# One fused image-and-text transformer block on one core: the opening's transfers and first products, a bank in the expert loop, and the last tile's way to the result

## The reference

```
h = concat(class_token, patches @ W.T + b) + pos_embed      # 16 x 197 x 192
h = concat(h, txt)                                         # 16 x 325 x 192
q, k, v = split(layernorm(h) @ W_qkv + b_qkv)
h = h + ((q @ k.T) / sqrt(192) * decay_mask) @ v
y = layernorm(h)                                           # 5200 rows
sig = sigmoid(y @ Wg.T)                                    # 128 experts
top 6 of sig + e_bias per row; weights sig / sum * 2.5
expert e takes at most its first 192 rows:
  routed += w * ((silu(y @ gate_e) * (y @ up_e)) @ down_e) # inner width 464
shared = (silu(y @ Wsg) * (y @ Wsu)) @ Wsd                 # inner width 928
result = h + routed + shared
```

## Time and profile before

| | us |
|---|---|
| median of 3 runs | 711.11 |
| the profiled execution's own time | 710.25 |
| its span, first to last instruction | 708.6 |
| TensorE busy in the span | 675.0 (95%) |
| VectorE (DVE) busy | 471.5 (67%) |
| ScalarE (ACT) busy | 331.9 (47%) |
| GpSimd (POOL) busy | 210.5 (30%) |
| mean granted TensorE clock | 0.988 |

### The profile page before, as it was taken

The page is one execution under the profiler, slowest core; times in us unless marked ns, Lnnn a source line. Parts: engine busy times, 40 slices in busy tenths (PEclk is TensorE's granted clock), DMA queues, the critical chain, the costliest instruction groups (busy, mean ns, idle before and its releaser), DMA issues.

```text
span 708.6 us, 16559 instructions
## 1 busy us (share of the span) xinstructions
PE 675.0 (95%) x4587; PEld 630.5 (89%) x4588; DVE 471.5 (67%) x1486; ACT 331.9 (47%) x803; POOL 210.5 (30%) x312
## 2 busy tenths in 40 slices
PE   6979999999999999999999999999999999999993
PEld 6879988999989888889999999999999999999993
DVE  2357788887888888666576666666666666666651
ACT  1335555645556565444444444444444444444431
POOL 3113223232233300310333333333333324242430
PEclk9989999999999999999999999999999999999998
DMA  8136344544444232621454544445464545454531
GB/s 280 44 101 218 112 131 144 172 131 136 145 136 144 88 104 54 181 71 25 99 110 99 110 99 102 108 99 111 97 113 97 113 97 113 97 113 97 113 56 20
DMA packets 74180, 79.36 MB, mean 112 GB/s; under 512 B 6361, under 2 KB 65897, under 8 KB 74154
## 3 DMA queue, kind: packets, MB, share of 16 engines
q1 hardware_dynamic: 61706, 65.81, 33.1%
q0 software_dynamic: 12160, 12.60, 11.0%
q10 hardware_dynamic: 288, 0.66, 0.3%
HBM read 51.73 MB, written 19.32 MB: 100 GB/s over the span
## 4 chain that ended last, share of the span: by engine, by line
PE 67%; DVE 12%; DMA 8%; issue 7%; ACT 2%; POOL 1%; DVEq 1%; POOLq 0%; ACTq 0%; SPq 0%
PE bank L1220 19%; PE bank L1030 9%; PE bank L1190 9%; PE bank L1239 7%; PE bank L1018 6%; PE bank L1202 6%; DMA result<-y_rows,put_idx 5%; PE bank L1060 3%; PE bank L1240 3%; DMA result<-s_rows 1%; DVE s_inter L1657 1%; DVE stats L1387 1%; PE bank L1088 1%; DVE w_raw L1483 1%; DVE h L1411 1%
## 5 line engine op out<-in xcount | busy, mean ns | idle before, releaser
L1657 DVE TENSOR_TENSOR s_inter<-s_gate,bank 128x384 f32<-128x384 f32 (+1 forms) x112 | 60.3, 539 | 68.7 <-PE bank L1220 58.8
L1239 PE MATMUL bank<-s_dn,s_in_hi 128*128 128x384 f32 (+1 forms) x287 | 87.3, 365 | 3.3 <-DVE s_rows L1672 3.0
L865 ACT ACTIVATE s_gate<-bank 128x384 f32<-128x384 f32 (+1 forms) x112 | 53.5, 479 | 67.7 <-PE bank L1220 67.7
L1030 PE MATMUL bank<-w_tok,patches 128*128 128x192 f32 x384 | 72.7, 343 | 8.2 <-DMA patches<-xp 6.9
L689 POOL DMA_INDIRECT result<-y_rows,put_idx x40 | 65.4, 1635 | 38.1 <-DVE y_rows L1644 15.3
L1220 PE MATMUL bank<-all_hiA,s_hi 128*128 (+4 forms) x210 | 73.5, 350 | 2.0 <-DVE s_inter L1657 0.6
L760 ACT ACTIVATE y<-h,shift,rstd 128x192 f32<-128x192 f32 (+2 forms) x96 | 45.6, 538 | 59.4 <-POOL shift L623 59.4
L1030 PEld LDWEIGHTS bank<-w_tok,patches 128*128 128x128 f32 x384 | 65.7, 200 | 8.1 <-issue 8.1
L1240 PE MATMUL bank<-s_dn,s_in_lo 128*128 128x192 f32 (+1 forms) x287 | 72.0, 251 | 0.0
L1220 PE MATMUL bank<-all_B,s_lo 128*128 (+4 forms) x210 | 70.1, 334 | 0.0
L1220 PE MATMUL bank<-all_B,s_hi 128*128 (+4 forms) x210 | 70.1, 334 | 0.0
(11 more groups left out here) (205 smaller groups left out, 1846.4 us busy)
## 6 DMA issues: line engine op xcount, KB each, us to landing
raw_gu<-wgu SPq DMA_DIRECT2D x22, 464.0 KB, 5.0
raw_gu<-wgu SPq DMA_DIRECT2D x44, 232.0 KB, 5.9
patches<-xp SPq DMA_DIRECT2D x16, 588.0 KB, 4.4
down_w<-wdn SPq DMA_DIRECT2D x22, 348.0 KB
result<-s_rows POOLq DMA_DIRECT2D x13, 288.0 KB
result<-h SPq DMA_DIRECT2D x16, 192.0 KB
yw_rows<-y SPq DMA_DIRECT2D x16, 192.0 KB
all_hiA<-y_hiA SPq DMA_DIRECT2D x16, 162.5 KB, 2.6
```

The lines of the kernel that those rows point to most:

```text
L865: act.activation(s_gate[m % 2][0:r, 0:width], up_banks(m, alone)[0][0:r, 0:width], ACT.Silu).then_inc(s_gate_ready, 1)
L1030: mm = pe.matmul(tok_ps[:, t * D:(t + 1) * D], own[:, c, t * 128:(t + 1) * 128], w_tok[:, c, :], start=c == 0, stop=c == KC - 1)
L1239: pe.matmul(bank[0:r, 0:2 * D], s_in_hi[:, m, rows], s_dn[:, m, :], start=m == 0, stop=False)
L1657: dve.tensor_tensor(s_inter[m % 2][0:r, 0:width], s_gate[m % 2][0:r, 0:width], up, ALU.mult).then_inc(s_inter_ready, 1)
```

## The change

Opening: patches and weights of sequence 0 come in three pieces each, and each piece has its own semaphore; `first` is cut in three (query and key part, value part, value bias); the text rows of sequences 0 and 1 go straight into `h0` and into `addend` and a new tile `addend_1`, all issued before `patches_1`; patches of sequence 2 are issued before `late`; `base` moves to ACT's queue. TensorE runs ten products of a zeroed tile before the first data. In step 0 ACT evicts the query ahead of norm 2, TensorE does the attention product ahead of the turning, and POOL copies the text ahead of its norm arithmetic. Loop: tile 1 of `s_down` uses bank 6 (`su_ps`), the first half of `down` moves ahead of `count_rows` and `s_up` 4, `weigh` moves behind `s_lo_part` 4, `slot_images` behind `s_lo_part` 5. Drain: SP loads the chunk's rows of the result after all adds of the loop, TensorE adds them to the down product with an identity matmul, each of the three tiles has a bank of its own, and SP stores each tile with a plain transfer.

```diff
+PAIRS = KC // 2
+WARM = 10
...
+        added_rows = Region(from_end).place("added_rows", [128, TILES, D])
+        tok_0_ps = (psum[0][:, 0:D], psum[5][:, 0:D])
...
         def down_bank(t, alone):
-            if alone and t % 2:
-                return psum[2] if alone == PACKED else dn_ps
+            if alone == END:
+                return (psum[7], psum[3], psum[2])[t]
+            if t % 2:
+                return psum[2] if alone == PACKED else dn_ps if alone else su_ps
             return sd_ps
...
-                load(0)
-                sp.dma_start(base[:, :, :], c_base).then_inc(base_in, 16)
-                sp.dma_start(first[:, :], w_first).then_inc(first_in, 16)
+                for i in range(PAIRS):
+                    pair = slice(2 * i, 2 * i + 2)
+                    sp.dma_start(patches[:, pair, 1:IMG], xp[0, :, pair, :]).then_inc(patch_0_in[i], 16)
+                sp.dma_start(first[0:96, 0:2 * QK_COLS], w_first[0:96, 0:2 * QK_COLS]).then_inc(wqk_in, 16)
+                sp.dma_start(addend[IMG - 128:128, 1, :], txt[0, 0:256 - IMG, :]).then_inc(t1_in, 16)
+                for n in range(2):
+                    sp.dma_start(h0[0:TL[2], 3 * n + 2, :], txt[n, 256 - IMG:TXT, :]).then_inc(text_in[n], 16)
+                sp.dma_start(addend_1[IMG - 128:128, :], txt[1, 0:256 - IMG, :]).then_inc(t1_1_in, 16)
                 sp.dma_start(patches_1[:, :, 1:IMG], xp[1, :, :, :]).then_inc(patch_1_in, 16)
+                load_patches(2)
                 sp.dma_start(late[:, :], c_late).then_inc(late_in, 16)
+                sp.dma_start(first[:, FIRST - 2 * D:FIRST], w_first[:, FIRST - 2 * D:FIRST]).then_inc(bv_in, 16)
                 sp.dma_start(cum32, c_cum).then_inc(cum_in, 16)
-                load_patches(2)
-                load_text(1)
...
+                first_k, more_k = load_first(sp, act_n), load_more(sp, act_n)
+                wait_apart(sp, passed, (gu_split, pairs * 4 + 2), (added, pairs * PER_PAIR + ADDED_AHEAD))
+                with sp.Fori(first_k, BEHIND) as k:
+                    rows = acc[bass.ds(k * WIDTH + BASE, WIDTH), :].rearrange("(t p) n -> p t n", p=128)
+                    before_k = (k + more_k) * TILES + AHEAD_TILES
+                    wait_apart(sp, passed, (sd_mm, before_k))
+                    sp.dma_start(added_rows[:, :, :], rows).then_inc(added_in, 16)
+                    for t in range(TILES):
+                        wait_apart(sp, passed, (s_rows_ready, before_k + t + 1))
+                        sp.dma_start(rows[:, t, :], s_rows[:, t, :]).then_inc(stored, 16)
...
-                act.dma_start(w_tok[:, :, :], wtok).then_inc(w_in, 16)
+                for i in range(PAIRS):
+                    pair = slice(2 * i, 2 * i + 2)
+                    act.dma_start(w_tok[:, pair, :], wtok[:, pair, :]).then_inc(w_in[i], 16)
+                act.dma_start(base[:, :, :], c_base).then_inc(base_in, 16)
+                act.dma_start(first[:, 2 * QK_COLS:FIRST - 2 * D], w_first[:, 2 * QK_COLS:FIRST - 2 * D]).then_inc(wv_in, 16)
...
-                    normed(n2, h1, n)
+                    if not isinstance(n, int) or n > 0:
+                        normed(n2, h1, n)
                     if more:
                         q_evac(n + 1)
+                    if isinstance(n, int) and n == 0:
+                        normed(n2, h1, n)
...
+                    if begun:
+                        attend(n + 1)
                     turn(n2, n)
-                    if more:
+                    if more and not begun:
                         attend(n + 1)
...
-                for t in range(2):
-                    tokens(0, t)
+                for i in range(PAIRS):
+                    pe.wait_ge(w_in[i], 16)
+                    pe.wait_ge(patch_0_in[i], 16)
+                    for t in range(2):
+                        for c in range(2 * i, 2 * i + 2):
+                            mm = pe.matmul(tok_0_ps[t], patches[:, c, t * 128:(t + 1) * 128],
+                                           w_tok[:, c, :], start=c == 0, stop=c == KC - 1)
...
+                    if m == 0 and not isinstance(o, int):
+                        wait_apart(pe, passed, (s_rows_ready, tiles_before(o) - 1))
...
-                    if not alone or t == 0:
-                        wait(pe, s_rows_ready, tiles_before(o) + t)
-                    elif t > 1:
-                        pe.wait_ge(s_rows_ready, tiles_before(o) + t - 1)
+                    if t != 1 and (alone != END or t == 0):
+                        wait(pe, s_rows_ready, tiles_before(o) + max(t - 1, 0))
...
+                def s_add(t, loads):
+                    if t == 0:
+                        pe.wait_ge(added_in, loads)
+                    pe.matmul(down_bank(t, END)[:, 0:D], ident[:, :], added_rows[:, t, :],
+                              start=False, stop=True).then_inc(sd_mm, 1)
...
+                        if t > 0:
+                            s_add(t - 1, loads)
+                    s_add(tiles - 1, loads)
...
                     turn_rows(j, 1)
+                    down(j, 0, 0)
                     count_rows(j, 3, 0)
                     s_up(o, data, WIDTH, 4)
-                    down(j, 0, 0)
...
-                    slot_images(j, 4)
+                    gated(j, 1, 0)
+                    s_mul(o, WIDTH, 5)
+                    s_lo_part(o, WIDTH, 4)
                     weigh(j, 0)
-                    gated(j, 1, 0)
-                    s_lo_part(o, WIDTH, 4)
-                    s_mul(o, WIDTH, 5)
                     gu_low(j, 2, 0)
                     gated(j, 1, 1)
                     s_mul(o, WIDTH, 6)
                     s_lo_part(o, WIDTH, 5)
+                    slot_images(j, 4)
```

More of the change, by code:

```diff
@@ L302, in build @@
         passed = sem("passed")
-        w_in = sem("w_in")
+        w_in = [sem(f"w_in{i}") for i in range(PAIRS)]
+        patch_0_in = [sem(f"patch_0_in{i}") for i in range(PAIRS)]
+        text_in = [sem(f"text_in{i}") for i in range(2)]
+        t1_1_in = sem("t1_1_in")
         base_in = sem("base_in")
         base_set = sem("base_set")
-        first_in = sem("first_in")
+        wqk_in = sem("wqk_in")
+        wv_in = sem("wv_in")
+        bv_in = sem("bv_in")
+        warm_set = sem("warm_set")
         ident_in = sem("ident_in")
@@ L1124, in step @@
                         score(n + 1)
+                    if begun:
+                        attend(n + 1)
                     turn(n2, n)
[L1126 removed]
+                    if more and not begun:
                         attend(n + 1)
                     logits(n)
[L1130 removed]
+                pe.wait_ge(warm_set, 1)
+                for i in range(WARM):
+                    pe.matmul(psum[7][:, 0:D], q_A[:, 0:128], q_A[:, 128:128 + D], start=True, stop=True)
                 pe.wait_ge(pool_set, 1)
[L1132 to L1134 removed]
+                for i in range(PAIRS):
[5 more added lines that the diff above has]
+                                           w_tok[:, c, :], start=c == 0, stop=c == KC - 1)
+                mm.then_inc(tok_mm, 1)
+                pe.wait_ge(wqk_in, 16)
                 for h in range(2):
@@ L1245, in s_down, with s_alone @@
                         pe.wait_ge(s_end_ready, o + 1)
-                    pe.matmul(bank[0:r, 0:D], s_last[:, rows], s_dl[:, :], start=False, stop=True).then_inc(sd_mm, 1)
+                    mm = pe.matmul(bank[0:r, 0:D], s_last[:, rows], s_dl[:, :], start=False, stop=alone != END)
+                    if alone != END:
+                        mm.then_inc(sd_mm, 1)
+                def s_add(t, loads):
[3 more added lines that the diff above has]
+                              start=False, stop=True).then_inc(sd_mm, 1)
                 def moving(at, width):
                     return [big[:, bass.ds(at, width)] for big in (all_hiA, all_loA, all_B)]
-                def s_alone(o, at, width, tiles, rows_out):
+                def s_alone(o, at, width, tiles, rows_out, loads):
                     data = moving(at, width)
@@ L1409, in token_rows @@
                     dve.wait_ge(tok_mm, n + 1)
-                    dve.wait_ge(t1_in, 16 * n + 16)
-                    dve.tensor_tensor(h0[:, bass.ds((n % 2) * 3, 2), :], tok_ps[:, 0:2 * D].rearrange("p (t c) -> p t c", t=2),
-                                      addend[:, :, :], ALU.add).then_inc(h0_ready, 1)
-                    wait_apart(dve, passed, (h0_ready, n + 1), (h0_txt, n + 1))
+                    if isinstance(n, int) and n == 0:
+                        dve.wait_ge(t1_in, 16)
+                        for t in range(2):
+                            ins = dve.tensor_tensor(h0[:, t, :], tok_0_ps[t], addend[:, t, :], ALU.add)
+                        ins.then_inc(h0_ready, 1)
+                    elif isinstance(n, int) and n == 1:
+                        dve.wait_ge(t1_1_in, 16)
+                        dve.tensor_tensor(h0[:, 3, :], tok_ps[:, 0:D], addend[:, 0, :], ALU.add)
```

(9 more changed lines are left out.)

56 lines of the change are left out of this document (34 added, 22 removed).

## The result

The changed kernel takes 699.2 us (median of four runs, 696.5 to 699.4), the kernel before 710.3 (a fourth run, of 709.5, moves its median down from 711.1); the ratio is 0.984 with a 95% interval of 0.981 to 0.987. 701.5 had been forecast, 694.5 to 706.5 as the range. The profiled executions are 710.25 and 699.24 us, their spans 708.6 and 697.4, so 11.2 us have to be found.

| part | before | after | gained | forecast |
|---|---|---|---|---|
| up to the loop | 318.1 | 318.7 | -0.6 | 1.6 |
| loop, ten rounds | 359.3 | 353.9 | 5.4 | 5.3 |
| drain, to the span's end | 31.15 | 24.8 | 6.4 | 2.0 |

The account below looks back on a forecast made before the run. TensorE's own order was taken as the bound. From 710.25 us, gains of 1.6 (opening), 5.3 (loop) and 2.0 (drain) gave 701.35, stated as 701.5, with a range of 694.5 to 706.5.

Parts of the forecast that it names:

- Bank: Loop: `s_down` tile 1 in bank 6 no longer waits 0.30 us a round; with pipeline restart 3.5 us gained.
- order: Loop: half of `down` ahead of `s_up` 4 covers its wait, 2.1 us gained; DVE's new order charged 0.03 a round.
- Opening, transfers: Opening: text rows ahead of `patches_1` cost +3.1 us, value bias moved behind saves 0.5; landing at 17.3 us.
- Opening, TensorE: Opening: zero products end at 4.4, sequence 0's tokens at 9.6, then 5.9 us idle; first score product 1.9 us later.
- Opening, step 0: Step 0: query evicted right behind its product, removing most of TensorE's 3.67 us idle; 3.5 us gained (bounds 2 and 5).
- in return the clock does not fall: Step 0: without the idle gap, products behind it run at full clock, 12 of them 1.3 us shorter.
- the tail: End of kernel: about 4.6 us from the plain store's landing to the last instruction.
- The other terms: Drain: plain store gains 2.7 us; three identity products cost 0.5 and loaded rows 0.2; 2.0 net (bounds -1 and 3).
- (A): Opening: text rows cost only their bytes, `patches_1` in by 14.5, clock stays up; 693.5 us, chance 0.14.
- (B): Loop: bank's gain handed back, `s_up` 7 waiting for `s_mul` 6 or DVE's list being longer; 705.5 us, chance 0.14.
- (C): Loop: slower, DVE's list decides the round, with `weigh` in front of `gu_low`; 715 us, chance 0.06.
- (D): Drain: row load comes late, TensorE waits 2 us at the first identity product; 703.4 us, chance 0.1.

Follow-up runs that it names:

- text_split: Changed kernel with each of the four early text transfers split into 48 + 11 and 64 + 5 rows: 691.5 us, ratio 0.973.
- no_zero_products: Changed kernel without the ten zero products, all else the same: 700.2 us, ratio 0.986.
- split_fill: Changed kernel with early text rows split, plus 17 unread products in two idle places of TensorE in step 0: 692.5 us, ratio 0.975.
- p1_first: Changed kernel with the two text transfers of sequence 1 issued behind `patches_1` instead of ahead: 695.4 us, ratio 0.977.

## Why the prediction was right, and where it was not

**Loop: right.** Bank 3.5 forecast, 3.6 measured; order 2.1 - 0.3 = 1.8 forecast, 1.6 measured. What was late next was only the next matmul.

**Opening, transfers: right in the number, half right in the mechanism.** `patches_1` at 17.3 forecast, 17.0 measured. The rule of the Trainium skill on which it leaned (page "DMA: Bandwidth & Descriptors", section "Why a DMA increments its semaphore by 16 and not by 1") agrees with the trace, in which 69 rows land in three parts and 59 in one, and with text_split, where pieces of 48 and 64 rows land in sixteen and the last sixteenth of `patches_1` is no longer late. But I had taken every transfer behind the text rows to land 3.1 us later as a whole; in the kernel before most of it was the last part alone (of `base` 10.98 against 8.45 for the other 15). What came on top with the change is SP's blocked issue (4.12 us), which was not in the forecast. That +2.6 was forecast and +2.2 measured is in part luck.

**Opening, TensorE: the zero products were mis-sized.** "Ten zero products from about 1.5 us at 0.29 each end at 4.4": they are 20 instructions of 0.29, and end at 7.0. Tokens of sequence 0 are done at 11.0 instead of 9.6, the gap ahead of sequence 1 is 4.0 instead of 5.9 us. It cost nothing, as no_zero_products shows, because `patches_1` is later than either. First score product +2.15 against the forecast's +1.9.

**Opening, step 0: the gain came, and went.** 3.5 forecast; 2.15 behind at the score, 1.15 ahead at the turning behind the first logits, so 3.3. But "in return the clock does not fall" failed: the two waits that took the old one's place (1.4 ahead of the attention product, of which 1.1 was forecast, and 1.9 ahead of the logits, which was not) leave TensorE idle from 43.1 to 44.5 and from 47.3 to 49.1 us, and the clock falls at 50.4, where it fell at 43.1 before. With those two waits filled it did not fall (split_fill). It costs the turning and the tokens (0.56 + 0.54 + 2.92) - (0.31 + 0.28 + 2.00) = 1.4 us. With the 2.15: 3.3 - 2.15 - 1.4 = -0.3, and 0.3 more is lost up to the loop. So the opening gave -0.6 and not 1.6.

**Drain: the tail was mis-sized, and this is the largest error.** The forecast kept "about 4.6 us (708.6 less 704) from its landing to the last instruction". It is POOL's closing instruction, which follows POOL's last landing by 4.0 us; since SP stores the last rows, 0.3 us are left. The other terms: 2.7 forecast for the transfer, 698.74 to 704.3 before and 694.83 to 697.1 after, 5.56 - 2.27 = 3.3 measured. Against it 0.7 forecast, measured 22.2 - 21.3 = 0.9 from the loop's end to the end of the last sum: the identity products are six instructions of 0.17, not three, and the loaded rows were there (issued at 687.57, landed at 690.5, wanted at 690.8). 3.3 + 4.0 - 0.9 = 6.4.

So 699.2 lies 2.3 under the forecast: 4.4 more from the drain, 2.2 less from the opening. Two errors of opposite sign met in one sum, and that the total came so near is luck: the drain's 6.4 lies far outside its own bounds (-1 to 3). The range was wide enough for each error by itself.

**Rivals.** (A), the opening's gain comes through, is what text_split does, at 691.5; what stood against it, 3.1 us for 96 KB, was measured as 2.5 on `base`. (B) and (C) did not happen: no wait at `s_up` 7, and DVE's list had the slack. (D) did not happen.

## What to carry to other kernels

Read the last instructions of every engine before pricing a tail: an interval between the last landing and the end of the span belongs to some engine, and it goes if that engine's last transfer comes early. Count instructions in the trace, not calls in the code, for each kind of product: here that was missed for the zero products, the identity products and the filler, and each was twice as long as planned. A transfer whose number of rows spreads badly costs those behind it, and the queue that issues them, more than itself; splitting it into a part that spreads and a small rest was worth up to 2.5 us alone and opened 5 more.

## What was not expected of the hardware

- POOL's closing instruction ended 4.0 and 4.1 us behind the landing of POOL's last transfer where it ended the span (8.4 and 5.7 us long), and 4.1 us behind it, off the path, in the kernel after (8.6 us long). SP's lasted 7 ns.
- An issue on SP's queue took 4.12 us behind transfers of 59 and 69 rows, 3.35 in p1_first for the 69 rows issued behind `patches_1`, and 0.4 to 0.6 with those rows in pieces of 48, 11, 64 and 5.
- Seventeen products that nobody reads (34 instructions), put where TensorE would wait, kept its granted clock at 1.00 in two traces where it was 0.50 without them, and yet the median did not fall: they outlasted the waits by 1.8 us.
